# Three multi-head attentions: queries and keys projected transposed for four batches and spread by transfers to 64 rows a head

## The reference

```python
# layer 0
x = LN(x + self_attention_with_past(x))   # 16 heads of 8; past: 2 states of 256 keys
x = LN(x + cross_attention(x, ctx))       # 16 heads of 8, block of 128, local plus windowed: twice the same here
x = LN(x + experts(x))                    # 16 routed, 2 shared
# layer 1
x = LN(gated_unit(x)); x = LN(x + one_head_attention(x, ctx)); x = LN(x + top1_experts(x))
```

## Time and profile before

| | us |
|---|---|
| median of three runs | 910.84 (896.62 to 913.6) |
| span of the profiled execution | 910.4 |
| PE, PEld, DVE, ACT, POOL busy | 734.9, 450.3, 639.3, 453.4, 93.6 |

### The profile page before, as it was taken

One profiled execution on the slowest core, in us unless ns is written; L12 is line 12 of the kernel. 1 busy time (PEld: TensorE's weight loads), 2 busy tenths in 40 slices (PEclk: granted clock), 3 DMA queues, 4 the chain that ended last, 5 costly groups with the idle time before them and its releaser, 6 DMA issues.

```text
span 910.4 us, 19336 instructions
## 1 busy us (share of the span) xinstructions
PE 734.9 (81%) x5976; PEld 450.3 (49%) x5980; DVE 639.3 (70%) x1605; ACT 453.4 (50%) x865; POOL 93.6 (10%) x212
## 2 busy tenths in 40 slices
PE   4888888779999999998488988649987766785674
PEld 2566665314444444444356656434433666564553
DVE  4788887588888888841478988565655688575455
ACT  2578887306777777776376677420000222343111
POOL 2000000500011110112100000010000232010000
PEclk8799999659999999999589999859999699895555
DMA  8300000000000000000000000000000000000001
GB/s 235 86 10 8 10 12 1 1 0 1 2 1 0 0 0 0 1 2 1 6 9 11 6 8 10 1 0 1 0 0 0 1 1 0 15 26 1 0 0 47
DMA packets 16222, 11.69 MB, mean 13 GB/s; under 512 B 3152, under 2 KB 15056, under 8 KB 16016
## 3 DMA queue, kind: packets, MB, share of 16 engines
q1 hardware_dynamic: 16176, 11.09, 4.4%
HBM read 10.04 MB, written 1.05 MB: 12 GB/s over the span
## 4 chain that ended last, share of the span: by engine, by line
PE 62%; DVE 20%; issue 10%; ACT 6%; DVEq 2%; POOL 0%; ACTq 0%; DMA 0%; SPq 0%; POOLq 0%
PE banks L870 8%; PE banks L840 8%; PE banks L858 6%; PE banks L1347 6%; PE banks L436 4%; PE banks L425 2%; DVE KT L616 2%; PE banks L404 2%; DVE KT L617 2%; PE banks L879 2%; PE banks L1409 2%; DVE negmax L1042 2%; PE banks L1676 2%; PE banks L1701 1%; PE banks L392 1%
## 5 line engine op out<-in xcount | busy, mean ns | idle before, releaser
L1042 DVE TENSOR_REDUCE negmax<-banks 128x2 bf16<-128x512 f32 x256 | 173.2, 696 | 33.9 <-PE banks L840 29.8
L978 ACT ACTIVATE probs<-banks 128x1024 f32<-128x1024 f32 x128 | 130.9, 1023 | 55.7 <-PE banks L858 54.5
L840 PE MATMUL banks<-shared 96*128 96x512 bf16 x256 | 108.4, 426 | 5.0 <-DVE negmax L1042 4.2
L624 DVE TENSOR_REDUCE negmax<-banks 128x4 bf16<-128x512 f32 x128 | 84.9, 686 | 13.3 <-PE banks L404 12.4
L870 PE MATMUL banks<-probs,rV 128*32 128x256 f32 x1024 | 82.2, 393 | 1.9 <-ACT o_T L985 1.3
L858 PE MATMUL banks<-shared 128*128 (+1 forms) x512 | 78.4, 276 | 1.9 <-ACT shared L989 1.9
L510 ACT ACTIVATE probs<-banks 128x512 f32<-128x512 f32 x128 | 73.0, 596 | 10.4 <-PE banks L425 9.8
L1347 PE MATMUL banks<-shared,w_r 128*128 128x512 f32 x128 | 64.4, 595 | 1.9 <-DVE shared L1380 1.8
L840 PEld LDWEIGHTS banks<-shared 96*128 (+1 forms) x256 | 25.1, 98 | 71.4 <-DVE negmax L1042 44.3
L1380 DVE TENSOR_TENSOR shared<-banks,out_T 128x512 f32<-128x512 f32 x64 | 43.6, 690 | 23.1 <-PE banks L1330 22.3
L436 PE MATMUL banks<-probs,V 128*32 128x128 f32 x1024 | 54.9, 287 | 4.5 <-ACT probs L510 3.4
(11 more groups left out here) (266 smaller groups left out, 1470.5 us busy)
## 6 DMA issues: line engine op xcount, KB each, us to landing
kv_T<-in_ctx_T SPq DMA_DIRECT2D x32, 64.0 KB, 1.7
x_T<-in_x_T SPq DMA_DIRECT2D x16, 64.0 KB, 1.8
w_r<-in_w_r SPq DMA_DIRECT2D x1, 1024.0 KB, 4.9
out<-Y SPq DMA_DIRECT2D x4, 256.0 KB, 2.4
shared<-in_past_rows SPq DMA_DIRECT2D x1, 512.0 KB, 4.6
gate_rows<-in_gate_rows SPq DMA_DIRECT2D x1, 512.0 KB, 6.0
past_T<-in_past_T SPq DMA_DIRECT2D x1, 256.0 KB, 2.6
KT<-in_head_rows SPq DMA_DIRECT2D x2, 128.0 KB, 3.2
```

The source lines that it names most:

```text
L624: nc.vector.tensor_reduce(c.negmax[:, u, 4 * k:4 * k + 4], c.max_banks[k % 2].rearrange("p (h t) -> p h t", h=4), AX_X, ALU.max, negate=Tr ...
L840: nc.tensor.matmul(c.max_banks[v], c.rQT[0:ROWS, h // 2, bass.ds(m * PAIR + v * P, P)], c.rKT[0:ROWS, h, :], start=True, stop=True).then_i ...
L978: nc.scalar.activation(c.probs[:, k % 4, :], c.score_pairs[k % 2], ACT.Exp, scale=HEAD_SCALE)\
L1042: nc.vector.tensor_reduce(out, c.max_banks[v].rearrange("p (a t) -> p a t", a=NP_PAST), AX_X, ALU.max, negate=True).then_inc(s["rec_max"], 1)
```

## The change

The queries and keys of four batches are projected in one product with the features on the partitions (`project_q`, `project_k`: weights as stationary operand, 512 tokens moving). The weights' columns are permuted on the host so that a feature's place is r x 64 + d x 8 + j for head 2j + r. ACT makes the high part with the bias (`high`), DVE the rest (`rest`), POOL the middle and low part (`middle_low_pool`; ACT and DVE for the first group). `spread_rows` on SP then writes each part by transfers from SBUF to SBUF to the rows slot + 8d of `QT` and `KT`, six transfers per projection. A head has 64 rows: 48 of parts, unused rows that are zero, and the last one or two for maxima and indicators. Even heads use rows 0 to 63, odd heads rows 64 to 127; their products stand next to each other in PE's order and write to different banks. No transposes of parts, no masks. The maxima are transposed to 16 (8) rows, cast by ACT (`copy_neg`), and sent by SP into row 63 (rows 62 and 63) of each half (`rows`).

Scores of a batch come in two halves of 8 heads: exp over 1024 columns, reductions over two banks, 1024 columns. V has its own product per batch. Output and rq projections are made for four batches at once from `out_T`. Past keys and values are computed during steps 2 and 3 of self attention. All loops of the three attentions are written out. `window(t)` on each engine places the group work. The past attention's maxima run 10 steps ahead (`LEAD`), nine of them during steps 16 to 18 of self attention; its maxima are handed over in quarters of a pair. The copy of `out` on POOL is gone. SP loads x for four batches at a time, then six weights, later all the others (`others(1)`), behind the first spreads and ahead of the first maximum row. `prepare_pe` and `prepare_dve` move into step 12.

```diff
-ROWS = SLOTS * 2 * HD
...
+GROUP = 4 * P
...
+Q_ORDER = (0, 0, 0, 1, 1, 2)
+K_ORDER = (0, 1, 2, 0, 1, 0)
...
+def high(c, act, name, g, bias, parts):
+    nc, s = c.nc, c.sem
+    act.wait_ge(*s.after(name + "proj", g + 1))
+    nc.scalar.activation(parts[:, 0, :], c.proj_bank, ACT.Identity, bias=bias).then_inc(s[name + "hi"], 1)
+def rest(c, dve, name, g, bias, parts, left):
+    nc, s = c.nc, c.sem
+    dve.wait_ge(*s.after(name + "hi", g + 1))
+    if g:
+        dve.wait_ge(*s.after(name + "lo", g))
+    nc.vector.scalar_tensor_tensor(left, c.proj_bank, bias, parts[:, 0, :], ALU.add, ALU.subtract)\
+        .then_inc(s[name + "rest"], 1)
+def middle_act(c, act, name, g, parts, left):
+    nc, s = c.nc, c.sem
+    act.wait_ge(*s.after(name + "rest", g + 1))
+    nc.scalar.copy(parts[:, 1, :], left).then_inc(s[name + "mid"], 1)
...
+def middle_low_pool(c, pool, name, g, parts, left):
+    s = c.sem
+    pool.wait_ge(*s.after(name + "rest", g + 1))
+    pool.tensor_copy(parts[:, 1, :], left).then_inc(s[name + "mid"], 1)
+    pool.wait_ge(*s.after(name + "mid", g + 1))
+    pool.tensor_tensor(parts[:, 2, :], left, parts[:, 1, :], ALU.subtract).then_inc(s[name + "lo"], 1)
+def spread_rows(c, sp, name, g, dst, parts, order, landed):
+    s = c.sem
+    for which, signal in enumerate(("hi", "mid", "lo")):
+        sp.wait_ge(*s.after(name + signal, g + 1))
+        for slot in range(SLOTS):
+            if order[slot] == which:
+                sp.dma_start(dst[slot:P:8], parts[:, which, :]).then_inc(s[landed], 16)
...
+    def max_scores(i, half):
+        g, gp, at_ = group_of(i)
+        if half == 0 and i % 4 == 0:
+            pe.wait_ge(*s.after(ph + "qt%d" % gp, 96 * (g // 2 + 1)))
+            pe.wait_ge(*s.after(ph + "kt%d" % gp, 96 * (g // 2 + 1)))
+        if half or i:
+            pe.wait_ge(*s.after(ph + "max", 2 * i + half))
+        for a in range(4):
+            for r in range(2):
+                j = 4 * half + a
+                last = nc.tensor.matmul(c.max_banks[r][:, a * P:(a + 1) * P], c.QT[64 * r:64 * r + 62, gp, j, at_:at_ + P],
+                                        c.KT[64 * r:64 * r + 62, gp, j, at_:at_ + P], start=True, stop=True)
+        last.then_inc(s[ph + "maxprod"], 1)
...
+        for a in range(4):
+            for r in range(2):
+                j = 4 * half + a
+                last = nc.tensor.matmul(c.score_banks[r][:, a * P:(a + 1) * P], c.KT[64 * r:64 * r + 64, gp, j, at_:at_ + P],
+                                        c.QT[64 * r:64 * r + 64, gp, j, at_:at_ + P], start=True, stop=True)
...
+        if t % 4 == 0 and t < 12:
+            project_q(t // 4 + 1, *([("past_v", 1)] if t == 4 else [("self_out", t // 4 - 1)] if t > 4 else [("self_k_rest", 1)]))
+        if t % 4 == 1 and t < 12:
+            project_k(t // 4 + 1, ("self_q_rest", t // 4 + 2))
+        if t == 2:
+            past_keys()
+        if t == 3:
+            past_values()
+        if t == 10:
+            project_rq(0, ("self_k_rest", 4))
+        if t == 12:
+            prepare_pe(c, pe)
+        if t == 14:
+            project_rq(1, ("prep_d", 1))
...
+    if cross:
+        project_k(0, ("rec_exp", 16 * NPAIR))
+        turn_x(0, ("cross_k_rest", 1))
+        project_q(0)
+        turn_x(1, ("cross_q_rest", 1))
+    else:
+        pe.wait_ge(*s.after("load_first", c.n_load_first * 16))
+        project_q(0)
+        project_k(0, ("self_q_rest", 1))
...
+    for t in range(LAST + (1 if cross else 0)):
+        if 0 <= t - 2 < B:
+            scores(t - 2, 0)
+        if t < B:
+            max_scores(t, 0)
+        if cross and 0 <= t - 4 < B:
+            cross_out(t - 4)
+        if 0 <= t - 3 < B:
+            turn_ctx(t - 3)
+        if 0 <= t - 2 < B:
+            values(t - 2, 0)
+            scores(t - 2, 1)
+        if t < B:
+            max_scores(t, 1)
+        if 0 <= t - 3 < B:
+            turn_norm(t - 3)
+        if t < B:
+            project_v(t)
+        window(t)
+        if 0 <= t - 2 < B:
+            values(t - 2, 1)
+        if t < B:
+            turn_max(t)
+        if more:
+            more(t)
...
+    def maximum(i, half):
+        dve.wait_ge(*s.after(ph + "maxprod", 2 * i + half + 1))
+        if half == 0 and i >= 2:
+            dve.wait_ge(*s.after(ph + "max_turned", i - 1))
+        nc.vector.tensor_reduce(c.negmax[:, i % 2, :].rearrange("p (r j) -> p r j", r=2)[:, :, 4 * half:4 * half + 4],
+                                c.max_pair.rearrange("p (r a t) -> p r a t", r=2, a=4), AX_X, ALU.max,
+                                negate=True).then_inc(s[ph + "max"], 1)
...
+    def load(g):
+        if g >= 3:
+            sp.wait_ge(*s.after(ph + "v_proj", 4 * (g - 3) + 4))
+            sp.wait_ge(*s.after(ph + "k_proj", g - 2))
+        sp.dma_start(c.xk_T[:, g % 3, :].rearrange("p (b t) -> p b t", b=4),
+                     x_T[4 * g:4 * g + 4].rearrange("b p t -> p b t")).then_inc(s[ph + "x%d" % (g % 3)], 16)
+    def queries(g):
+        if g >= 2:
+            sp.wait_ge(*s.after(ph + "score", 8 * (g - 1)))
+        elif cross:
+            sp.wait_ge(*s.after("rec_score", 4 * STEPS * (g + 3)))
+        spread_rows(c, sp, ph + "q_", g, c.QT[:, g % 2], c.qk_parts[:, 0], Q_ORDER, ph + "qt%d" % (g % 2))
+    def keys(g):
...
+        spread_rows(c, sp, ph + "k_", g, c.KT[:, g % 2], c.qk_parts[:, 1], K_ORDER, ph + "kt%d" % (g % 2))
+    def rows(i):
+        g, gp, at_ = group_of(i)
+        sp.wait_ge(*s.after(ph + "neg", i + 1))
+        sp.dma_start(c.QT[63:P:64, gp, :, at_:at_ + P], c.neg_T[:, i % 2, :]).then_inc(s[ph + "negd%d" % (i % 2)], 16)
+    load(0)
+    if not cross:
+        others(0)
+    load(1)
+    load(2)
+    if cross:
+        keys(0)
+        queries(0)
+    else:
+        sp.wait_ge(*s.after("set_zero", 2))
+        queries(0)
+        keys(0)
+        others(1)
+    for t in range(B + 2):
+        if 0 <= t - 1 < B:
+            rows(t - 1)
+        if t % 4 == 2 and t < 12:
+            queries(t // 4 + 1)
+        if t % 4 == 3 and t < 12:
+            keys(t // 4 + 1)
+        if t == 4:
+            load(3)
+        if t == 14 and not cross:
+            past_queries_sp(c, sp, 0)
+        if not cross and t == 4:
+            spread_rows(c, sp, "past_", 0, c.rKT, c.rq_parts[:, 3], K_ORDER, "past_kt")
...
+class PastPE:
...
+        self.nc.tensor.matmul(c.max_banks[r], c.QT[64 * r:64 * r + 62, g % 2, j, off:off + P],
+                              c.rKT[64 * r:64 * r + 62, j, :], start=True, stop=True).then_inc(s["rec_maxprod"], 1)
...
+        for a in range(2):
+            last = self.nc.tensor.matmul(c.score_pairs[i % 2][:, r * 512 + a * PAIR:r * 512 + (a + 1) * PAIR],
+                                         c.rKT[64 * r:64 * r + 64, 2 * g + a, t * P:(t + 1) * P],
+                                         c.QT[64 * r:64 * r + 64, (n // 2) % 2, 2 * g + a,
+                                              (n % 2) * PAIR:(n % 2 + 1) * PAIR], start=True, stop=True)
+        last.then_inc(s["rec_score"], 1)
...
+    def run(self):
+        self.lead(LEAD - self.ahead)
+        self.turn_max(0, 0)
+        for n in range(NPAIR):
+            for k in range(STEPS):
+                i = STEPS * n + k
+                more = self.ahead < ALL_STEPS
+                self.scores(n, k, 1)
+                if more:
+                    self.max_scores(self.ahead, 0)
+                if i:
+                    self.values((i - 1) // STEPS, (i - 1) % STEPS)
+                self.scores(n, k, 0)
+                if more:
+                    self.max_scores(self.ahead, 1)
+                    self.ahead += 1
+                if i == 0:
+                    self.turn_max(0, 1)
+                if k == 2 and n:
+                    self.turn_ctx(n - 1, 3)
+                if k in (3, 7):
+                    self.turn_max(n, k // 4 + 2)
+                if k == 5 and n:
+                    self.turn_sum(n - 1)
+                if k in (6, 10, 14):
+                    self.turn_ctx(n, k // 4 - 1)
+                if k == 9 and n:
+                    self.gate_product(n - 1)
+                if k in (11, 15) and n + 1 < NPAIR:
+                    self.turn_max(n + 1, k // 4 - 2)
+                if k == 13 and n:
+                    self.turn_out(n - 1)
...
+    def rows(n, q):
+        sp.wait_ge(*s.after("rec_neg", 4 * n + q + 1))
+        off = (n % 2) * PAIR
+        for past in range(NP_PAST):
+            sp.dma_start(c.QT[62 + past:P:64, (n // 2) % 2, 2 * q:2 * q + 2, off:off + PAIR],
+                         c.rec_neg_T[4 * past:4 * past + 4, q, :]).then_inc(s["rec_negd%d" % q], 16)
```

More of the change, by code:

```diff
@@ L35 @@
 HV = 32
+GROUP = 4 * P
+NGROUP = B * P // GROUP
 NE = 16
@@ new lines, in values @@
+    def values(i, half):
+        pe.wait_ge(*s.after(ph + "exp", 2 * i + half + 1))
+        if half == 0:
+            pe.wait_ge(*s.after(ph + "v", i + 1))
+            if i:
+                pe.wait_ge(*s.after(ph + "ctx", i))
+            elif not cross:
```

(70 more changed lines are left out.)

1224 lines of the change are left out of this document (583 added, 641 removed).

## The result

The changed kernel takes 915.89 us (median of 22 runs, 910.06 to 935.89) where the kernel before took 912.91 (22 runs, 895.1 to 914.95). The ratio is 1.019, 95% interval 1.015 to 1.023; it leaves out runs over 1.5% above the fastest of their kernel, and so compares with only three runs of the kernel before (895 to 897), while the medians have a ratio of 1.003. Whether the changed kernel is slower at all is therefore open; it is not faster. The forecast was 797, in a range from 750 to 855. The profiled execution of the changed kernel is its slowest, 935.89 us with a span of 934.1; so I go by stages, not by its total.

The account below looks back on a forecast made before the run. No engine was full, so the order of work set the pace, with PE bounding the past loop. From 910.8 us it took 57 (start), 19 (past loop) and 38 (cross), giving 797, range 750 to 855.

Parts of the forecast that it names:

- The past loop: Past attention: score and maximum products of different row halves run side by side, step 1.6 us, 203 against 222: -19 us.
- DVE at 93% and PE near 80%: Sign of the forecast in the past loop: these busy shares at 1.6 us a step.
- the 98%: Past loop sign: PE's busy share stays near 98% if row halves take turns.
- Taking turns: Rival: row halves take turns and each array shape change costs 0.15 us; past step 2.0, total 853; chance 10%.
- The clock: Rival: TensorE's clock falls to 1.2 GHz in eight-head stages and past loop; 926 with past loop untouched; chance 4%.
- under 0.9 in the loops: Sign that the forecast is wrong: the granted clock falls below 0.9 in the loops.
- The start: Up to the first past score: self scores begin at about 41, first past scores at 146 instead of 203.3: -57 us.
- the hand-over: Rival in self and cross attention: SP's spreads and rows wait behind each other; step 6.5, total 837; chance 16%.
- Cross: Cross attention: filling, 14 steps of mean 5.3 us and a tail of 16, together 108 against 146: -38 us.
- between them: Chain from the past loop's last score to cross attention: loses a POOL copy beside other work, 0 us.
- the rest: Layer 2 and the experts, 585 to 910 us, keep their instructions: 0 us.

Follow-up runs that it names:

- normalising alone: Changed kernel with values behind all score and maximum products of a past step and DVE normalising before its first maximum: 804.2 us, ratio 0.878.
- values last: Changed kernel with a past step's values moved behind all its score and maximum products: 819.53 us, ratio 0.902.
- the old kernel with the new order: Kernel before the change, two of four score products per past step moved behind the values of the step before: 975.03 us, ratio 1.076.
- keys and normalising: Changed kernel with values behind all score and maximum products, key parts sent in the queries' step, and DVE normalising before its first maximum: 805.5 us.
- the later loads: Changed kernel with 21 of 47 weight loads moved behind the first maximum rows, four in each of the next steps: 912.56 us, ratio 1.007.

## Why the prediction was wrong

**The failed step** is in "The past loop": "PE needs 0.57 + 2 x 0.27 = 1.11 us a step", for DVE 1.52, "I take 1.6". I priced each engine's work and took the larger; I never followed one exp to the next through the new order. Taking the rows that I had: exp 1.02, values 0.57 to the next start, and the wait from the first of the last two score products to exp 0.43 and from exp to values 0.06, both as measured after, make 2.08 at full clock. That is over the 1.79 before, and it is the 2.07 to 2.08 that both kernels with this order show. The diff showed it: `values` between `scores(n, k, 1)` and `scores(n, k, 0)`. In self attention values stand between the two halves of the scores as well, but there I traced the chain (scores, exp, values) and put its wait into the sum; in the past loop I did not. None of my rivals held it. The ring, with the clock that fell along with it, is worth 97 of the 119 us between forecast and result.

**The size of that step was also off.** With the ring gone, PE's six products take 0.54 as forecast, and values 0.58. But the step then is 1.73 us, against the 1.6 in which I had included that "four transposes a pair now wait for DVE's normalise". That wait was real and cost more than I gave it: only with DVE's normalising first, which the changed kernel doesn't have, is the step 1.59. That this gives 203.1 us, the forecast 203, is luck. The busy shares came out the other way round too: I had named DVE at 93% and PE near 80%, and in that fastest loop (160 to 347 of the kernel with normalising alone) PE's records cover 98% and DVE's 88%. So the 98% that I gave as the mark of halves taking turns doesn't tell the two cases apart.

**Taking turns** (10%, 853) is refuted: the pairs start together, and the loop with its ring removed takes 1.73 us a step, not 2.0. The Trainium skill (TensorEngine Tiling (Array Packing), Key Properties) says that different tiles can load weights and multiply in parallel. The trace agrees: two starts at 252.81, and 0.54 us where the six products in 96 and 128 rows took 0.97.

**The clock** (4%) was 0.94 in the self window, 0.81 in cross, 0.82 to 0.85 in the past loop and 0.53 in the loop's end behind the maxima, so my sign "under 0.9 in the loops" did appear. In the past loop it was a consequence and not the origin: with the same instructions and values last it is 1.00 from 165 to 290. Yet the stall alone doesn't lower it: the old kernel with the new order has 1.00 from 205 to 395. Why it fell in the one and not in the other is open.

**The start** (forecast 146 to the first past score, measured 160.6) was mis-sized in three terms. The first self score was due at 41 and came at 49.7: SP's timeline shows why.

```profile
10.08 9.85 SPq L381 DMA_DIRECT2D shared<-qk_parts  x12
...
42.41 0.81 SPq L2099 DMA_DIRECT2D Y<-in_x  x1
43.28 2.09 SPq L888 DMA_DIRECT2D shared<-neg_T  x2
45.42 4.17 SPq L381 DMA_DIRECT2D shared<-qk_parts  x6
```

A spread costs 9.85/12 = 0.82 us of issue, 4.17/6 = 0.70 later, and each of the first two maximum rows 1.05 (later single ones 0.55), where I took 0.43 from a plain weight load. So the list of loads began at 20.7, not at 14.5, and the first maximum row behind it was issued at 43.3, not at 34.7; the scores that need it began 6.5 us later, where I had allowed up to 6.0 for landing. The 14 steps behind it took 80.0 us (49.7 to 129.7), 5.7 a step against 5.4; the tail 30.9 against 29. The longest step of self attention, 8.7 us, is at a group border, and in cross the three border steps take 7.2 to 9.8 where the others take 4.3 to 6.1; there PE stands idle ahead of the first maximum products of the new group, by up to 3.4 us. That fits the hand-over that I had at 16% as a rival; it came in mild form. Landing of a spread was 2.4, taken 2.2, and the reduction over 1024 columns 1.22, taken 1.25:

```profile
shared<-qk_parts SPq DMA_DIRECT2D x96, 128.0 KB, 2.4
...
L745 DVE TENSOR_REDUCE negmax<-banks 128x8 bf16<-128x1024 f32 x64 | 78.3, 1223 | 86.1 <-PE banks L443 86.0
```

**Cross** was 117.4, forecast 108: 22.0 instead of 17.7 to the first score (516.7), then 82.5 for 14 batches against 74, and 12.8 of tail against 16. With the keys' parts in the queries' step it takes 112.

Sum of the misses against the profiled time: start 14.6, past loop 115, cross 9.4, between them 2.1, the rest -3.2, and 1.8 instead of 0.4 around the span: together 139, which is 935.9 - 797.

## What to carry to other kernels

When an edit moves instructions within the step of a software pipeline, write out the ring for the new order: for each engine pair, what must end before the next pass of the slowest instruction can start. Busy totals give only a lower bound; the longest ring gives the plain step (2.08 by its terms, 2.07 measured), and the copies, transposes and the clock come on top (2.49 us on average in the changed kernel). Here one moved call is worth 97 us, and the sign of the whole change: with the order mended the same change is 10% faster than the kernel before, and with DVE's order changed too 12 to 13%.

## What the hardware showed that I had not expected

The last stage has two lengths in identical code. Its window of 63 us before the end, in the kernel with normalising alone and in the one with keys and normalising (columns as in the earlier trace rows):

```profile
731.80:794.80 63.00, 35.55 (x258) 29.00 (x256) 40.55 (x200) 14.51 (x46) 4.11 (x14) 0.83 0.06 17
```

```profile
741.30:804.30 63.00, 38.88 (x200) 33.44 (x200) 32.82 (x160) 11.03 (x34) 2.93 (x10) 0.53 0.06 17
```

In the same 63 us the first gets 258 matmuls done at a clock of 0.83, the other 200 at 0.53. From the statistics ahead of the stage to those behind it, profiles take 63.5 us (three kernels), 66 to 68 (two), or 79 to 80 (six, both the kernel before and the changed one among them). This shifts a total by 15 us without any cause in the edit, and would account for the runs of the kernel before, which fall at 895 to 898 or at 908 to 915; of these only one with a long last stage (80.2 us, span 910.4) was profiled. What decides between the two lengths I did not find out. It is larger than two of the effects above, the later loads and the keys' step, which totals don't resolve.
